# Whole fp32 rows and one fp32 weight in place of fp32r halves, in a three-layer graph network

## The reference, cut to what matters

```python
for Wl, bl, Wr, g, b in params:            # three layers, 20000 nodes x 512, 5000 edges
    msg = h[src]
    s = segment_sum(msg, dst)
    agg = s / maximum(cnt, 1.0)
    h = residual + agg @ Wl.T + bl + h @ Wr.T
    h = layer_norm(h, g, b)
    h = where(h >= 0, h, a_prelu * h)
    residual = h
out = layernorm(x + h)
```

## Time and profile before

| | |
|---|---|
| median of 3 runs | 2077.23 us (2076.5 to 2077.98) |
| the profiled execution | 2078.05 us, span 2076.2 us |
| TensorE busy | 1991.9 us (96%) |
| weight loads | 1653.8 us (80%) |
| VectorE, ScalarE, GpSimd busy | 1539.4, 1206.4, 1513.0 us |
| granted TensorE clock, mean | 0.986 |
| HBM traffic | 387.7 MB, 187 GB/s |

### The profile page before, as it was taken

How to read it: one execution, slowest core, us unless ns; L and a number is a source line. 1 busy time by engine, 2 the same in 40 slices (tenths; PEclk the granted TensorE clock), 3 DMA queues, 4 the chain that set the end, 5 groups by cost and what they waited for, 6 DMA issues and landing times. The chain is left out here.

```text
span 2076.2 us, 30403 instructions
## 1 busy us (share of the span) xinstructions
PE 1991.9 (96%) x10149; PEld 1653.8 (80%) x10149; DVE 1539.4 (74%) x2382; ACT 1206.4 (58%) x2643; POOL 1513.0 (73%) x1122
## 2 busy tenths in 40 slices
PE   6999999999999999999999999999899999999992
PEld 4777888788888888888888888887778888888882
DVE  6556676667567655666666666669999999999994
ACT  3774455445444455544444444458877777777774
POOL 2788888888888766655555555558878888888886
PEclk8999999999999999999999999999999999999996
DMA  5566676566666654544444444455666666666652
GB/s 182 180 209 231 201 233 213 193 223 205 207 210 206 188 160 174 173 150 149 150 150 148 149 152 153 142 168 198 220 213 209 211 213 209 203 207 208 200 190 89
DMA packets 181073, 387.66 MB, mean 187 GB/s; under 512 B 20117, under 2 KB 20562, under 8 KB 180918
## 3 DMA queue, kind: packets, MB, share of 16 engines
q1 hardware_dynamic: 142358, 272.06, 38.9%
q0 software_dynamic: 38560, 113.67, 17.2%
HBM read 221.07 MB, written 164.79 MB: 186 GB/s over the span
## 5 line engine op out<-in xcount | busy, mean ns | idle before, releaser
L393 PE MATMUL ps_z<-w_hi,hT_hi 128*128 128x512 f32 x1884 | 764.1, 406 | 11.1 <-ACT ps_z L519 10.5
L662 POOL TENSOR_TENSOR y<-y,shift 128x1024 f32<-128x1024 f32 (+1 forms) x237 | 614.4, 2592 | 172.2 <-DVE y L767 169.4
L393 PE MATMUL ps_z<-w_hi,hT_lo 128*128 128x512 f32 x1884 | 739.9, 393 | 0.0
L393 PE MATMUL ps_z<-w_lo,hT_hi 128*128 128x512 f32 x1884 | 739.1, 392 | 0.0
L519 ACT COPY ps_z<-bias_rows 128x512 f32<-128x512 f32 x471 | 276.4, 587 | 459.6 <-DVE y L767 402.5
L755 DVE TENSOR_TENSOR hT_lo<-ps_t,hT_hi 128x1024 fp32r<-128x1024 f32 (+1 forms) x237 | 287.5, 1213 | 328.9 <-ACT hT_hi L490 328.3
L393 PEld LDWEIGHTS ps_z<-w_hi,hT_hi 128*128 128x128 f32 x1884 | 355.4, 189 | 83.3 <-issue 16.1
L393 PEld LDWEIGHTS ps_z<-w_hi,hT_lo 128*128 128x128 f32 x1884 | 354.2, 188 | 79.4
L499 ACT ACTIVATE junk<-ps_z 128x512 f32<-128x512 f32 x471 | 277.5, 590 | 229.2 <-PE ps_z L393 223.7
L393 PEld LDWEIGHTS ps_z<-w_lo,hT_hi 128*128 128x128 f32 x1884 | 355.6, 189 | 67.3
L767 DVE SCALAR_TENSOR_TENSOR y<-ps_z,rstd,gain 128x512 f32<-128x512 f32 x471 | 330.2, 742 | 57.0 <-POOL rstd L650 57.0
(11 more groups left out here) (131 smaller groups left out, 1974.4 us busy)
## 6 DMA issues: line engine op xcount, KB each, us to landing
h_scratch<-hout SPq DMA_DIRECT2D x156, 512.0 KB
hin<-h_scratch SPq DMA_DIRECT2D x156, 512.0 KB, 3.8
x_by_slot<-hin SPq DMA_DIRECT2D x78, 512.0 KB
o_sb<-x_by_slot SPq DMA_DIRECT2D x78, 512.0 KB
rowtab<-edge_row_table SPq DMA_DIRECT2D x60, 256.0 KB
stage<-in_WrT SPq DMA_DIRECT2D x3, 1024.0 KB
stage<-in_WlT SPq DMA_DIRECT2D x3, 1024.0 KB
hin<-in_x,node_get POOLq DMA_INDIRECT x157
```

The costliest lines, as they stand in the source:

```text
L393: mm = pe.matmul(acc, a[:, k, :], ww[:, k, :], start=False, skip_group_check=True, stop=stop and k == KC - 1 and a is a_lo)
L662: nc.gpsimd.tensor_tensor(y[u.r2][:, 0:u.n, :], y[u.r2][:, 0:u.n, :], moved, ALU.add).then_inc(shifted, 1)
```

## The change

TensorE multiplies the plain fp32 transposed rows by one centred fp32 weight, one `matmul` call a chunk (`product`), in place of three on halves. `hT_lo`, `w_lo`, `sT_hi` and `sT_lo` go, with the instructions that made them; ScalarE's copy of the transposed rows is now fp32 and alone frees `ps_t`; `product_mean` reads `sumT` itself, so that the wait for the products of the unit of messages before moves from ScalarE's copy into VectorE's `carry`. VectorE adds the shift, in place of GpSimd, for all units of the first layer and for every second one of the third (`here`). The matmuls of the sign tiles wait for the sixth row step once.

```diff
+    def here(no):
+        l, pos = divmod(no, UL)
+        return l == 0 or l == L - 1 and pos % 2 == 0
...
-            w_hi[w], w_lo[w] = sb(f"w_hi{w}", wide, F32R), sb(f"w_lo{w}", wide, F32R)
+            w_sb[w] = sb(f"w{w}", wide)
...
-        hT_hi = [sb(f"hT_hi{i}", [P, 2, KC, P], F32R) for i in range(2)]
-        hT_lo = [sb(f"hT_lo{i}", [P, 2, KC, P], F32R) for i in range(2)]
+        hT = [sb(f"hT{i}", [P, 2, KC, P]) for i in range(2)]
...
-                reach(pe, low, u.no)
+                reach(pe, taken, u.no)
...
-            def mm3(acc, a_hi, a_lo, w, stop):
+            def product(acc, a, w, stop):
                 for k in range(KC):
-                    for a, ww in ((a_hi, w_hi[w]), (a_hi, w_lo[w]), (a_lo, w_hi[w])):
-                        mm = pe.matmul(acc, a[:, k, :], ww[:, k, :], start=False, skip_group_check=True,
-                                       stop=stop and k == KC - 1 and a is a_lo)
+                    mm = pe.matmul(acc, a[:, k, :], w_sb[w][:, k, :], start=False, skip_group_check=True,
+                                   stop=stop and k == KC - 1)
...
-                pe.wait_ge(e_low, 2 * u.eno + j + 1)
-                mm3(ps_z[u.r2][:, j, :], sT_hi[j], sT_lo[j], 2 * u.l + 1, True).then_inc(z_ready, 1)
+                pe.wait_ge(e_carry, 2 * u.eno + j + 1)
+                product(ps_z[u.r2][:, j, :], sumT[j], 2 * u.l + 1, True).then_inc(z_ready, 1)
...
                         if i == 0:
                             pe.wait_ge(table_done, 1)
+                            pe.wait_ge(row_step, 6)
...
-            def take_sum_high(u, j):
-                act.wait_ge(e_carry, 2 * u.eno + j + 1)
-                if u.eno > 0:
-                    before = Unit(EDGE_AT[u.eno - 1])
-                    act.wait_ge(z_ready, before.ahead + j + 1)
-                nc.scalar.copy(sT_hi[j][:], sumT[j][:]).then_inc(e_high, 1)
...
             def add_shift(u):
-                if u.no == 0:
+                if u.here:
+                    return
+                if u.shifts == 1:
                     pool.wait_ge(affine_signed, 1)
...
-            def take_low(u):
-                dve.wait_ge(high, u.no + 1)
-                nc.vector.tensor_tensor(hT_lo[...], ps_t[...], hT_hi[...], ALU.subtract).then_inc(low, 1)
...
+            def add_shift_here(u):
+                if not u.here:
+                    return
+                dve.wait_ge(gained, u.upto)
+                moved = shift[:, u.l:u.l + 1, :].to_broadcast([P, u.n, D])
+                nc.vector.tensor_tensor(y[u.r2][:, 0:u.n, :], y[u.r2][:, 0:u.n, :], moved, ALU.add).then_inc(shifted_here, 1)
...
             def prelu(u):
-                dve.wait_ge(shifted, u.no + 1)
+                dve.wait_ge(shifted_here if u.here else shifted, u.shifts)
...
             def carry(u, j):
                 dve.wait_ge(e_summed, 2 * u.eno + j + 1)
+                if u.eno > 0:
+                    before = Unit(EDGE_AT[u.eno - 1])
+                    dve.wait_ge(z_ready, before.ahead + j + 1)
...
-                    take_low(ahead)
...
                     normal(last)
+                    add_shift_here(last)
...
-                        split_weight(w, T - at)
```

More of the change, by code:

```diff
@@ L68, in __init__ @@
             self.r2, self.r3 = no % 2, no % 3
+            self.here = here(no)
+            self.shifts = len([n for n in range(no + 1) if here(n) == self.here])
             self.eno = len(edge_units) * self.l + self.tiles[0] // 2
@@ L93, in build_program @@
         wide = [P, KC, D]
-        w_hi, w_lo = [None] * (2 * L), [None] * (2 * L)
+        w_sb = [None] * (2 * L)
         for w in range(2, 2 * L):
-            w_hi[w], w_lo[w] = sb(f"w_hi{w}", wide, F32R), sb(f"w_lo{w}", wide, F32R)
+            w_sb[w] = sb(f"w{w}", wide)
         stage = sb("stage", wide)
@@ L130, in build_program @@
         sumT = [sb(f"sumT{i}", [P, KC, P]) for i in range(2)]
-        sT_hi = [sb(f"sT_hi{i}", [P, KC, P], F32R) for i in range(2)]
-        sT_lo = [sb(f"sT_lo{i}", [P, KC, P], F32R) for i in range(2)]
         edge_cols = sb("edge_cols", [P, 3, ET], I32)
@@ L186, in build_program @@
         for w in range(2):
-            w_hi[w], w_lo[w] = sb(f"w_hi{w}", wide, F32R, early), sb(f"w_lo{w}", wide, F32R, early)
+            w_sb[w] = sb(f"w{w}", wide, where=early)
         early.close()
@@ L226, in build_program @@
         cols_in, rows_in, affine_in, bias_in = sem("cols_in"), sem("rows_in"), sem("affine_in"), sem("bias_in")
-        stage_in, w_mean, w_high, w_low, w_diag, w_signed = (
-            sem("stage_in"), sem("w_mean"), sem("w_high"), sem("w_low"), sem("w_diag"), sem("w_signed"))
+        stage_in, w_mean, w_moved, w_diag, w_signed = (
+            sem("stage_in"), sem("w_mean"), sem("w_moved"), sem("w_diag"), sem("w_signed"))
         bias_mean, bias_moved, seeded, filled = sem("bias_mean"), sem("bias_moved"), sem("seeded"), sem("filled")
@@ L240, in build_program @@
         h_stored = [sem(f"h_stored{i}") for i in range(3)]
-        turned, high, low, z_ready = sem("turned"), sem("high"), sem("low"), sem("z_ready")
+        turned, taken, z_ready = sem("turned"), sem("taken"), sem("z_ready")
         squared, veps_done, rstd_done = sem("squared"), sem("veps_done"), sem("rstd_done")
-        gained, shifted, h_done, affine_signed = sem("gained"), sem("shifted"), sem("h_done"), sem("affine_signed")
+        gained, shifted, shifted_here, h_done, affine_signed = (
+            sem("gained"), sem("shifted"), sem("shifted_here"), sem("h_done"), sem("affine_signed"))
         rt_in = sem("rt_in")
         m_in = [sem(f"m_in{j}") for j in range(2)]
-        e_same, e_summed, e_carry, e_high, e_low = (
-            sem("e_same"), sem("e_summed"), sem("e_carry"), sem("e_high"), sem("e_low"))
+        e_same, e_summed, e_carry = sem("e_same"), sem("e_summed"), sem("e_carry")
         xr_in = [sem(f"xr_in{i}") for i in range(OB)]
@@ L261, in load_weight @@
                 if w > 0:
-                    sp.wait_ge(w_low, KC * w)
+                    sp.wait_ge(w_moved, KC * w)
                 sp.dma_start(stage[:], wT[w].rearrange("(c p) k -> p c k", p=P)).then_inc(stage_in, 16)
@@ L400, in product_self @@
                 if j == 0:
-                    pe.wait_ge(low, u.no + 1)
+                    pe.wait_ge(taken, u.no + 1)
                     if u.pos == 0:
-                        pe.wait_ge(w_low, KC * (2 * u.l + 1))
+                        pe.wait_ge(w_moved, KC * (2 * u.l + 1))
                 pe.wait_ge(filled, u.ahead + j + 1)
-                mm = mm3(ps_z[u.r2][:, j, :], hT_hi[u.r2][:, j], hT_lo[u.r2][:, j], 2 * u.l, not u.edge)
+                mm = product(ps_z[u.r2][:, j, :], hT[u.r2][:, j], 2 * u.l, not u.edge)
                 if not u.edge:
@@ L412, in product_mean @@
                 if u.tiles[0] == 0 and j == 0:
-                    pe.wait_ge(w_low, KC * (2 * u.l + 2))
-                pe.wait_ge(e_low, 2 * u.eno + j + 1)
-                mm3(ps_z[u.r2][:, j, :], sT_hi[j], sT_lo[j], 2 * u.l + 1, True).then_inc(z_ready, 1)
+                    pe.wait_ge(w_moved, KC * (2 * u.l + 2))
+                pe.wait_ge(e_carry, 2 * u.eno + j + 1)
+                product(ps_z[u.r2][:, j, :], sumT[j], 2 * u.l + 1, True).then_inc(z_ready, 1)
             def turn_table(parts):
@@ L477, in center @@
                 act.wait_ge(w_mean, KC * w + c + 1)
-                nc.scalar.activation(w_hi[w][:, c, :], stage[:, c, :], ACT.Identity,
-                                     bias=w_neg[:, c:c + 1]).then_inc(w_high, 1)
+                nc.scalar.activation(w_sb[w][:, c, :], stage[:, c, :], ACT.Identity,
+                                     bias=w_neg[:, c:c + 1]).then_inc(w_moved, 1)
             def center_bias(l):
@@ L485, in center_bias, with take @@
                 nc.scalar.activation(rows_, rows_, ACT.Identity, bias=mean).then_inc(bias_moved, 1)
-            def take_high(u):
+            def take(u):
                 act.wait_ge(turned, u.no + 1)
                 reach(act, z_ready, Unit(u.no - 2).upto if u.no >= 2 else 0)
-                nc.scalar.copy(hT_hi[u.r2][:, 0:u.n].rearrange("p j k n -> p (j k n)"),
-                               ps_t[:, 0:u.n, :].rearrange("p j d -> p (j d)")).then_inc(high, 1)
+                nc.scalar.copy(hT[u.r2][:, 0:u.n].rearrange("p j k n -> p (j k n)"),
+                               ps_t[:, 0:u.n, :].rearrange("p j d -> p (j d)")).then_inc(taken, 1)
             def square(u, j):
@@ L542, in out_square @@
                 if u.pos == 0:
-                    act.wait_ge(w_low, 2 * L * KC)
+                    act.wait_ge(w_moved, 2 * L * KC)
                 reach(act, veps_done, u.no + 2)
@@ L569, in scalar_program @@
                 if ahead.exists:
-                    take_high(ahead)
+                    take(ahead)
                 old = Unit(T - 4)
@@ L817, in carry @@
                 ins.then_inc(e_carry, 1)
[L819 to L823, removed]
             def out_sum(u):
```

(2 more changed lines are left out.)

15 lines of the change are left out of this document (removed).

## The result

The changed kernel takes 2418.48 us (median of 4, 2418.17 to 2419.56) against 2077.61 before on the same chip: 1.164 times as long, interval 1.162 to 1.166. The prediction was 2460, range 2420 to 2565. The profiled execution took 2419.56 us, span 2417.8.

A forecast was written before the change was run, and what follows sets the result against it. The prediction took TensorE's stream of instructions plus some 85 us to bound the kernel. From 2078 us, +417 for products and -35 for idle time regained gave 2460 us, range 2420 to 2565.

The forecast's parts named there:

- Two instructions at the price of two sweeps each: Changed products on TensorE: 4728 instructions replace 7092, each two sweeps of 0.2133 us for 512 columns; +417 us.
- L385's pair of records: Message sums of L385: 480 fp32 matmuls issued, 960 records in the trace, so one fp32 matmul is two instructions.
- the transposes of the earlier trace: Last of eight fp32 transposes: 128 columns took 0.11 us, two sweeps, where the next load would have allowed 0.07.
- the one-sweep rival: Changed products at one sweep per instruction, 0.2292 us in place of 0.432: about 1635 us in all; chance 0.07.
- 0.432 an instruction: Start distance of the changed products: 0.427 us for two sweeps plus L385's excess of 0.005.
- 1625 us for the products before: 7092 fp32r matmuls at 0.2292 us, the layers' mean taken as (0.2335 + 2 x 0.2271) / 3.
- Idle time of 35 us: TensorE idle time regained at the start and in the loop, the latter giving 27 us; together -35 us.
- the loop over the units has only 29.6 us of idle TensorE: Of 84.1 us idle, 36.1 lie behind the last matmul and 18.6 in the first 39 us.
- Its low end: Range's lower bound of 2420 us: 0.428 an instruction (-19) and the bounds of the idle terms (-20).
- The shifts on VectorE: 119 shifts gained by VectorE at 1.2 us each, 143 us, at most 399; beside TensorE, not binding.
- The carry's new wait: VectorE's carry waits for products of the unit of messages before; claimed never the last wait, so nothing lost.
- the wait on the row step: Wait for the sixth row step, in slot 1, claimed to come when that work is done.

The follow-up runs named there:

- the run with 256 columns: The changed kernel with each chunk's fp32 matmul cut into two of 256 columns: 2430.33 us.

## Why the prediction was right and wrong

- **What bounds it: right.** TensorE set the time before and sets it fully now. All other removed work was worth only the time that TensorE had lost to it.
- **Two instructions at the price of two sweeps each: right.** The chance of 0.75 stood on L385's pair of records and on the transposes of the earlier trace rows; the run with 256 columns measured two clocks a column. The Trainium skill, FP8 and Floating Point Precision, TensorE Precision Notes, with its four passes agrees with 2 x 0.429 us a chunk against four sweeps of 0.213; the one-sweep rival fell.
- **0.432 an instruction: the first mis-sized term.** "L385 is the only row of this kind of instruction": the kind was right and the size was not. Its 0.005 go with its 128 columns (probably by the weight load, which wasn't tested apart); with 512 they are 0.003. Measured 0.4294: 4728 x 0.0026 = 12 us too much.
- **1625 us for the products before:** the third layer's starts were not read and are 0.2283. Measured 1629: 4 us.
- **Idle time of 35 us: the second mis-sized term, and the larger.** Measured 59 us, a miss of 24. The step that failed was "the loop over the units has only 29.6 us of idle TensorE" (29.4 by its own terms). That number is span less busy time, although the prediction itself said that matmul rows overlap: a row's modelled end lies some 0.18 us behind the start of the next, so every wait looks that much shorter than it is, and a shorter one isn't seen at all. The step of 8.80 us shows 1.36 of the 1.88 us that it lost, the steps of some 12.0 us of the third layer's units with messages nothing of the 0.24 that they lost against the 11.79 of the second. The third layer gave some 22 us where the prediction had 11 for its beginning, the start and the first layer some 35 where it had the other 24, and the end 2 where it had none. Steps measured from transposes to transposes hold the loss; the three terms together make 12 + 4 + 24 = 40 us, and 2460 - 40 is the profiled 2420.
- **The range.** Its low end took 0.428 (-19) and 20 us more idle time regained. The idle term alone ended 24 below its middle, beyond its own bound, because that bound was drawn from the same hidden count as the middle.
- **The shifts on VectorE: right in price (1.24), and free as forecast.** Not foreseen: what taking them off GpSimd gives back, nothing that can be measured in this kernel and 32 us in the one before with all of them moved (26 with those of the change).
- **The carry's new wait and the wait on the row step: no sign of either.** The table of waits of TensorE in the changed kernel has no row from 190 us to the end.

## What to carry to other kernels

Price a matmul by the distance of starts at the shape it will have; the excess of a short one (0.005 at 128 columns) is not that of a long one (0.003 at 512). Three rounded products beat one whole fp32 product on TensorE here by 2 x 0.429 against 3 x 0.230 us a chunk, as long as the engines that make the halves have room. Read what a stage loses from step to step, not from idle rows of TensorE. And before moving work off a full VectorE to GpSimd, look how long VectorE's own instructions get while GpSimd runs, and whether VectorE waits for small steps that stand behind the moved work on GpSimd: here taking 237 additions back made the kernel faster.

## What the hardware showed that was not expected

- A VectorE instruction of 0.75 us lasted 3.02 beside a 128x1024 addition on GpSimd.
- Streaming fp32r, a weight that starts 32 bytes past a multiple of 64 costs 0.004 us per 512 columns (0.2333 to 0.2293). Whole fp32 products in the changed kernel, whose first layer's weights stand 32 bytes off too, are 0.429 apart in all layers (steps of 7.74 in the first as in the third).
- One of the two instructions of a whole fp32 matmul carries 0.003 us over its sweeps, an fp32r one 0.014 over one sweep. Why the second is larger wasn't tried.
